# Layer norm inside a software-pipelined transformer stage: statistics and root moved from GpSimd to VectorE, ScalarE's part moved within its tick, output stored by batch

## The reference

```python
h = _layernorm(x)
for l in range(6):
    h = h + attn_layer(shift_tokens(h), Wqkv[l], q_scale[l], k_scale[l], Wo[l])
    h = h + ffn_layer(shift_tokens(h), ln_g[l], ln_b[l], W1[l], b1[l], W2[l], b2[l])
x = x + h

def ffn_layer(x, g, bln, W1, b1, W2, b2):
    mu = x.mean(-1, keepdims=True)
    var = ((x - mu) ** 2).mean(-1, keepdims=True)
    xn = (x - mu) / jnp.sqrt(var + 1e-05) * g + bln
    a, gate = jnp.split(xn @ W1 + b1, 2, -1)
    return a * jax.nn.gelu(gate, approximate=False) @ W2 + b2
```

## Time and profile before

| what | value |
|---|---|
| median of 3 runs | 2961.94 us (2951.48 to 2964.03) |
| profiled execution, own time | 2952.71 us |
| its span | 2950.9 us |
| mean granted TensorE clock | 0.936 of full speed |
| busy: PE, DVE, ACT, POOL | 88%, 59%, 53%, 49% of the span |
| last stage | from about 1815 us to the end |

### The profile page before, as it was taken

One profiled execution on the slowest core, in us unless ns is written; L12 is line 12 of the kernel. 1 busy time (PEld: TensorE's weight loads), 2 busy tenths in 40 slices (PEclk: granted clock), 3 DMA queues, 4 the chain that ended last, 5 costly groups with the idle time before them and its releaser, 6 DMA issues. The chain is left out here.

```text
span 2950.9 us, 59262 instructions
## 1 busy us (share of the span) xinstructions
PE 2591.2 (88%) x20009; PEld 1660.6 (56%) x20009; DVE 1740.3 (59%) x3832; ACT 1562.2 (53%) x5035; POOL 1434.5 (49%) x2340
## 2 busy tenths in 40 slices
PE   5999978898989979776689996999999999999996
PEld 3455545465645646554445553566666666666664
DVE  3466656546657655555545555766666667666662
ACT  1455536525747646532245553666665666666663
POOL 0344434203536613300024443877787777877772
PEclk8799998998979999987779998999999999999998
DMA  2000000010000000000000001010101101001000
GB/s 68 1 0 0 0 8 2 12 32 5 2 4 2 2 32 0 5 1 8 2 26 0 0 0 57 16 34 19 30 24 28 33 20 30 26 26 34 20 23 8
DMA packets 45612, 47.16 MB, mean 16 GB/s; under 512 B 11899, under 2 KB 31365, under 8 KB 45382
## 3 DMA queue, kind: packets, MB, share of 16 engines
q1 hardware_dynamic: 45382, 44.18, 5.3%
HBM read 31.05 MB, written 0.52 MB: 11 GB/s over the span
## 5 line engine op out<-in xcount | busy, mean ns | idle before, releaser
L1025 POOL TENSOR_TENSOR l_probs<-l_probs,rowinv 128x512 f32<-128x512 f32 (+2 forms) x256 | 192.4, 772 | 569.8 <-DVE rowinv L1037 569.0
L1045 DVE TENSOR_REDUCE negmax<-scores 128x1 f32<-128x508 f32 (+4 forms) x512 | 212.8, 467 | 220.1 <-PE scores L922 180.3
L2237 ACT ACTIVATE net_probs<-bank,net_negmax 128x96 f32<-128x96 f32 x768 | 250.9, 339 | 167.4 <-DVE net_negmax L2380 167.2
L2380 DVE TENSOR_REDUCE net_negmax<-bank 128x4 f32<-128x384 f32 x192 | 107.0, 557 | 319.6 <-PE bank L2085 318.9
L1025 POOL TENSOR_TENSOR lora_probs<-lora_probs,rowinv 128x508 f32<-128x508 f32 (+1 forms) x256 | 149.5, 617 | 255.2 <-DVE rowinv L1037 255.2
L2301 POOL TENSOR_TENSOR net_rope<-net_rope,net_sin_parts 128x512 f32<-128x512 f32 x192 | 243.8, 1270 | 9.6 <-DVE net_sin_parts L2356 9.6
L2309 POOL TENSOR_TENSOR net_probs<-net_probs,net_inverse 128x384 f32<-128x384 f32 x192 | 158.6, 826 | 153.4 <-DVE net_inverse L2363 153.4
L990 ACT ACTIVATE l_probs<-scores,negmax 128x512 f32<-128x512 f32 (+2 forms) x256 | 139.5, 550 | 167.8 <-DVE negmax L1045 167.0
L124 DVE COPY turned<-flip 128x512 f32<-128x512 f32 (+3 forms) x280 | 163.0, 582 | 74.2 <-PE flip L949 64.7
L2319 POOL TENSOR_TENSOR net_rope<-net_rope,net_head_inv 128x512 f32<-128x512 f32 x192 | 201.1, 1047 | 0.0
L737 DVE TENSOR_REDUCE negmax<-scores 128x2 f32<-128x256 f32 (+2 forms) x192 | 157.7, 822 | 65.8 <-PE scores L645 36.4
(11 more groups left out here) (426 smaller groups left out, 6471.3 us busy)
## 6 DMA issues: line engine op xcount, KB each, us to landing
net_w_qkv<-in_L_ffn_Wqkv SPq DMA_DIRECT2D x12, 768.0 KB, 5.7
net_vals_between<-net_vals SPq DMA_DIRECT2D x48, 192.0 KB, 2.5
net_w_out<-in_L_ffn_Wo SPq DMA_DIRECT2D x6, 512.0 KB, 4.2
net_vals_between<-net_vals SPq DMA_DIRECT2D x48, 64.0 KB, 1.9
moe_w<-in_L_ffn_w13T SPq DMA_DIRECT2D x8, 256.0 KB, 2.7
net_w<-in_L_ffn_W SPq DMA_DIRECT2D x6, 341.0 KB
moe_w<-in_L_ffn_w2T SPq DMA_DIRECT2D x8, 128.0 KB, 2.3
ctx_tok<-in_ctx SPq DMA_DIRECT2D x1, 768.0 KB, 6.6
```

Of the source, the lines that this page charges most:

```text
L1025: last = nc.gpsimd.tensor_tensor(own, own, rowinv[:, u * tail + w:u * tail + w + 1].to_broadcast([P, k1 - k0]), ALU.mult)
L1045: last = nc.vector.tensor_reduce(negmax[:, u * tail + w:u * tail + w + 1], scores[:, 2 * qt + h, k0:k1], AX.X, ALU.max, negate=True)
L2237: last = nc.scalar.activation(prob_blocks(g)[:, w, :], score_blocks(g)[:, w, :], ACT.Exp, bias=maxima[:, g % 4, w:w + 1], accum_out=sums[: ...
```

## The change

VectorE takes the statistics in LATE itself, right behind the copy of the late half, and makes the inverse root there (`root_of_variance`: eleven small operations that wait for each other, then the shift). GpSimd's root of the norm goes. ScalarE's low copy in LATE and its normalising in ZT move ahead of the exponentials of their tick, behind values' copy. In the last four jobs VectorE adds each batch to `x` as soon as its last sum is made, and SyncE stores that batch; `add_all` and `store` behind the stream go. Left out of the diff below are the argument lists without `ln_sum`, and the semaphores `finished` and `sent`.

```diff
@@ -1916,8 +1915,9 @@
             summed, stored = signal("net_summed", G), signal("net_stored", G)
             out_made, out_added = signal("net_out_made", JOBS), signal("net_out_added", JOBS)
             low_moved, late_made, late_moved = signal("net_low_moved", JOBS), signal("net_late_made", JOBS), signal("net_late_moved", JOBS)
-            measured, gathered, spread_in = signal("net_measured", 2 * JOBS), signal("net_gathered", 2 * JOBS), signal("net_spread", 2 * JOBS)
-            ln_rooted, normed = signal("net_ln_rooted", ROOT_OPS * JOBS), signal("net_normed", 2 * JOBS)
+            measured, gathered = signal("net_measured", 2 * JOBS), signal("net_gathered", 2 * JOBS)
+            LN_OPS = 11
+            ln_rooted, normed = signal("net_ln_rooted", LN_OPS * JOBS), signal("net_normed", 2 * JOBS)
             ln_shifted = signal("net_ln_shifted", JOBS)
             z_turned, z_moved = signal("net_z_turned", JOBS), signal("net_z_moved", JOBS)
             gates_made, gates_moved = signal("net_gates_made", JOBS), signal("net_gates_moved", 3 * JOBS)
...
@@ -2032,6 +2033,11 @@
                         if n is not None and n % B == B - 1 and n < JOBS - 1:
                             sp.wait_ge(down_made.sem, down_made.at(0, n + 1))
                             ffn_weights_in(n // B + 1)
+                        if n is not None and n >= JOBS - B:
+                            b = n % B
+                            sp.wait_ge(finished.sem, finished.at(0, b + 1))
+                            sp.dma_start(out[b].rearrange("(t p) d -> p t d", p=P), x[:, QT * b:QT * (b + 1), :]).then_inc(sent.sem, 16)
+                    sp.wait_ge(sent.sem, sent.at(0, B))
 
                 @block.tensor
                 def _(pe):
...
@@ -2228,6 +2234,19 @@
                             square(u, 1, k_filled)
                             act.wait_ge(v_filled.sem, v_filled.at(0, u + 1))
                             copy("act", vals[:, m % 3, t, half_cols(c)], v_bank).then_inc(v_copied.sem, 1)
+                        n = at_tick(s, LATE, PER, JOBS)
+                        if n is not None:
+                            l, b = job(n)
+                            own = slice(QT * b, QT * (b + 1))
+                            act.wait_ge(out_added.sem, out_added.at(0, n + 1))
+                            copy("act", z[:, own, 0:half], xin[:, own, 0:half]).then_inc(low_moved.sem, 1)
+                        n = at_tick(s, ZT, PER, JOBS)
+                        if n is not None:
+                            l, b = job(n)
+                            act.wait_ge(ln_shifted.sem, ln_shifted.at(0, n + 1))
+                            for q in range(QT):
+                                own = z[:, QT * b + q, :]
+                                affine("act", own, own, ln_inv[:, q:q + 1], ln_shift[:, q:q + 1]).then_inc(normed.sem, 1)
                         g = s
                         if 0 <= g < G:
                             act.wait_ge(maxed.sem, maxed.at(0, g + 1))
...
@@ -2243,12 +2262,6 @@
 
                             until(act, scored, g - 1)
                             copy("act", qk_T[:, g % 2, :, :].rearrange("p s n -> p (s n)"), turn_bank).then_inc(copied["act"].sem, 1)
-                        n = at_tick(s, LATE, PER, JOBS)
-                        if n is not None:
-                            l, b = job(n)
-                            own = slice(QT * b, QT * (b + 1))
-                            act.wait_ge(out_added.sem, out_added.at(0, n + 1))
-                            copy("act", z[:, own, 0:half], xin[:, own, 0:half]).then_inc(low_moved.sem, 1)
                         m = at_tick(s, SHIFT, PER, JOBS)
                         if m is not None:
                             l, b = job(m)
...
@@ -2257,10 +2270,6 @@
                         n = at_tick(s, ZT, PER, JOBS)
                         if n is not None:
                             l, b = job(n)
-                            act.wait_ge(ln_shifted.sem, ln_shifted.at(0, n + 1))
-                            for q in range(QT):
-                                own = z[:, QT * b + q, :]
-                                affine("act", own, own, ln_inv[:, q:q + 1], ln_shift[:, q:q + 1]).then_inc(normed.sem, 1)
                             if b == 0:
                                 act.wait_ge(ffn_in.sem, ffn_in.at(l, FFN_LOADS))
                             act.wait_ge(z_turned.sem, z_turned.at(0, n + 1))
...
@@ -2321,12 +2330,6 @@
                         if j is not None:
                             pool.wait_ge(reduced.sem, reduced.at(0, 2 * j + 2))
                             inverse_root(pool, head_sums[:, j % 2, :], 1e-24, head_inv[:, j % 2, :], head_temp, rooted, ROOT_OPS * j)
-                        n = at_tick(s, LATE + 1, PER, JOBS)
-                        if n is not None:
-                            pool.wait_ge(spread_in.sem, spread_in.at(0, 2 * n + 2))
-                            inverse_root(pool, ln_sum[:, :], LN_EPS, ln_inv[:, :], ln_temp, ln_rooted, ROOT_OPS * n)
-                            pool.wait_ge(ln_rooted.sem, ln_rooted.at(0, ROOT_OPS * (n + 1)))
-                            nc.gpsimd.tensor_tensor(ln_shift[:, :], ln_shift[:, :], ln_inv[:, :], ALU.mult).then_inc(ln_shifted.sem, 1)
                         u = at_tick(s, PROJ + 1, 2, S)
                         if u is not None:
                             add_parts(u, 0)
...
@@ -2356,24 +2359,30 @@
                         nc.vector.tensor_tensor(sin_parts[:, (2 * u + s) % 4, :].rearrange("p (h f d) -> p h f d", f=2, d=DH // 2), swapped, table,
                                                 ALU.mult).then_inc(parted.sem, 1)
 
+                    def root_of_variance(dve, n):
+
+                        lower, y, t = ln_temp[:, 0, :], ln_temp[:, 1, :], ln_temp[:, 2, :]
+                        done = [LN_OPS * n]
+
+                        def then(ins):
+                            done[0] += 1
+                            ins.then_inc(ln_rooted.sem, 1)
+                            dve.wait_ge(ln_rooted.sem, ln_rooted.at(0, done[0]))
+                        then(nc.vector.tensor_scalar(lower, meanvar[:, 0:QT, 1], LN_EPS, -0.5, ALU.add, ALU.mult))
+                        then(nc.vector.tensor_scalar(y.bitcast(I32), lower.bitcast(I32), -0.5, ROOT_MAGIC, ALU.mult, ALU.add))
+                        for r in range(3):
+                            then(nc.vector.tensor_tensor(t, y, y, ALU.mult))
+                            then(nc.vector.tensor_tensor(t, t, lower, ALU.mult))
+                            then(nc.vector.scalar_tensor_tensor(y if r < 2 else ln_inv[:, :], t, 1.5, y, ALU.add, ALU.mult))
+                        assert done[0] == LN_OPS * (n + 1)
+
+                        nc.vector.scalar_tensor_tensor(ln_shift[:, :], meanvar[:, 0:QT, 0], -1.0, ln_inv[:, :], ALU.mult, ALU.mult).then_inc(ln_shifted.sem, 1)
+
                     for s in TICKS:
                         g = s - 1
                         if 0 <= g < G:
                             dve.wait_ge(exped.sem, exped.at(0, g + 1))
                             nc.vector.reciprocal(inverse[:, g % 4, :], sums[:, g % 4, :]).then_inc(inverted.sem, 1)
-                        n = at_tick(s, LATE + 1, PER, JOBS)
-                        if n is not None:
-                            l, b = job(n)
-                            dve.wait_ge(late_moved.sem, late_moved.at(0, n + 1))
-                            dve.wait_ge(low_moved.sem, low_moved.at(0, n + 1))
-                            for q in range(QT):
-                                nc.vector.bn_stats(stats[:, q, :], z[:, QT * b + q, :]).then_inc(measured.sem, 1)
-                            for q in range(QT):
-                                dve.wait_ge(measured.sem, measured.at(0, 2 * n + q + 1))
-                                nc.vector.bn_aggr(meanvar[:, q, :], stats[:, q, :]).then_inc(gathered.sem, 1)
-                            dve.wait_ge(gathered.sem, gathered.at(0, 2 * n + 2))
-                            nc.vector.tensor_scalar(ln_sum[:, :], meanvar[:, 0:QT, 1], LN_EPS, None, ALU.add).then_inc(spread_in.sem, 1)
-                            nc.vector.tensor_scalar(ln_shift[:, :], meanvar[:, 0:QT, 0], -1.0, None, ALU.mult).then_inc(spread_in.sem, 1)
                         g = s
                         if 0 <= g < G:
                             dve.wait_ge(scored.sem, scored.at(0, g + 1))
...
@@ -2426,6 +2435,15 @@
                             l, b = job(n)
                             dve.wait_ge(late_made.sem, late_made.at(0, n + 1))
                             copy("dve", z[:, QT * b:QT * (b + 1), half:D], spare[:, 0:D].rearrange("p (t d) -> p t d", t=QT)).then_inc(late_moved.sem, 1)
+                            dve.wait_ge(late_moved.sem, late_moved.at(0, n + 1))
+                            dve.wait_ge(low_moved.sem, low_moved.at(0, n + 1))
+                            for q in range(QT):
```

(27 more changed lines are left out.)

## The result

The changed kernel takes 2929.24 us (median of 5 runs, 2919.78 to 2932.97) and the kernel before 2960.11 (5 runs, 2951.48 to 2964.03): a ratio of 0.9894, interval 0.9876 to 0.9911. The change makes the kernel 1.1% faster, some 31 us, where I had forecast 2967 and no measurable change. 2929 lies near the low end of my range. The profiled execution took 2919.78 us against 2952.71 before.

The account below looks back on a forecast made before the run. TensorE sets the pace, stalled 2.41 us in 22 jobs by ScalarE's normalising. Stall exchange +7.5, clock +9.4 and tail -4 make +13 on 2952.71, so 2965.6; stated as 2967 us, range 2922 to 2984.

Parts of the forecast that it names:

- The old stall: TensorE's transposes of the normed rows wait 2.41 us per job for ScalarE's normalising; ScalarE's new order alone removes this.
- the end of GpSimd's root: GpSimd loses the norm's root, some 4.2 us; costed at nothing, as TensorE doesn't wait for it in the steady part.
- The new one: TensorE stalls 2.75 us at values' projection (L2072), released by ScalarE's copy of the heads; +0.34 us per job net.
- The hold: A small root operation on VectorE waits for GpSimd's 1.27 us addition, making the maximum 2.87 us late instead of 1.7.
- ScalarE did not become second: Rival: exponentials behind the normalising delay the `qk_T` copy, so TensorE stalls twice a job; 2986 us, chance 0.18.
- The tail: Last job and end: earlier root 2.0 us, smaller sum and store 2.4, job 22 giving back up to 0.5; together -4.
- the store: At the end, last sum and store of one batch instead of four: gain between 1.7 and 3 us, taken as 2.4.
- VectorE's lateness: The root's chain on VectorE makes the next maximum 2.87 us late with the hold, 1.7 us without.
- the clock: TensorE's clock drops behind the stall in 16 of 22 jobs instead of 10, at 1.57 us each: +9.4 us.
- not held: Rival: VectorE's chain is not held behind GpSimd's addition, maximum only 1.7 us late; 2924 us, chance 0.27.

Follow-up runs that it names:

- the kernel with the addition first: Changed kernel with GpSimd's addition of the rotary parts placed ahead of the heads' inverse norms: 2902.97 us, ratio 0.9794 to the kernel before.
- the repeat: The changed kernel measured once more, without a further edit, beside the second group of runs: 2929.91 us, ratio 0.9901 to the kernel before.
- the kernel with four steps: Changed kernel with a fourth Newton step in the root, three more dependent operations on VectorE: 2990.88 us, ratio 1.0114 to the kernel before.

## Why the prediction was wrong

**What held.** The old stall went, but not as I had it: I wrote that ScalarE's order alone takes it away and costed the end of GpSimd's root at nothing. That order alone left 2.15 us of 2.41; it takes the earlier root as well. The change has both, so this error did not move the forecast. The new one came at values' projection, by ScalarE's copy of the heads, behind VectorE's maximum, once in each job and instead of the old one. The hold came in all 22 jobs. The Trainium skill, "SBUF — State Buffer", section "SBUF: two separate sides", has VectorE and GpSimd exclude each other for a whole instruction where VectorE's has two SBUF inputs and GpSimd's reads SBUF; here 22 of 22 chains show it, and the kernel with the addition first shows its price. ScalarE did not become second: the interval less the stall is 44.23 - 2.08 = 42.15 us, and 44.50 - 2.41 = 42.09 before, so no second wait of any size has come. The tail gave -7.4 where I had -4: ScalarE starts 2.36 us behind the root's first operation, not 2.54, and the store gave 3.0, above my 2.4 but within its bound; jobs 21 to 22 gave 1.5 where I allowed 0.5. That total leans on an undisturbed clock: in the repeat, with a drop between jobs 22 and 23, the tail gave only -3.2.

**The first wrong size: VectorE's lateness.** I had 2.87 us behind an old start, so a stall of 2.75 and +0.34 per job, +7.5 in all. (The sum's own rows make 2323.62 - 2320.77 = 2.85; the 0.02 doesn't matter.) The stall is 2.08 (2.24 in the seven jobs in which the third operation is held, as I had it), and the interval without a drop is shorter by 0.27 (by 0.11 in those), -4.8 in all. Measured on job 9 against the earlier trace rows, with the two executions laid on each other at the tick before (17.02 us apart), the maximum is late by 2.24, not 2.87. The parts are: the copy of `z` starts 0.16 earlier; a dependent step is 0.197 us and not 0.21, -0.14 over the chain; one operation more is through before GpSimd's addition begins (the fourth is held, not the third), -0.2; and the maximum starts 0.17 behind the last of the chain, not 0.27, -0.10. None is large; together they are 0.6 us, and turn the sign. The 0.34 was the difference of two stalls of 2.4 and 2.75, and the errors of the terms in it were 0.1 to 0.2 each.

**The second, and larger: the clock.** I took ten drops in 22 at 2.41 us, put "between 10 and 22" at 2.75 and added 9.4 us. With the stall at 2.08 the clock gave back some 12.6 in the profiled execution: 2 jobs of 22 have a drop instead of 10, for 0.3 us less stall. The term's slope was right in sign and far too flat. The table shows a steep place: 0 to 3 jobs of 22 with a drop up to 2.24 us, 10 at 2.41, 21 at 2.68, and there most cost 2.9 us. With my own stall of 2.75 the time would have been no 2967: the kernel with four steps has 2.68 and takes 2990.88. So 2967 was also wrong for the stall that it assumed. What the term needed was to be priced at both ends of the stall's uncertainty; the sign of the whole hung on whether the stall came out above or below the old one.

**The range.** 2922 to 2984 held 2929 by luck: only because the rival "not held" had its place near there, by another mechanism: the chain is held, and the time comes from a shorter lateness and from the clock.

**Open.** How many drops the timed runs have isn't seen; the two profiled executions have 2 and 3. Jobs 0 to 21 and the tail together give -27.1 and -21.1 us in these, against medians of -31 and -25; where the rest lies isn't shown. That a smaller stall goes with fewer drops is shown by every row of the table, with the stall at either of the two places. Why one of the same length is followed by a drop in some jobs and not in others was not tried. Nor was the 7.5 us between the starts of the stage.

## What to carry to other kernels

When an edit exchanges one stall for another of nearly its size, the difference is what must be worked out, and everything that hangs on it by a steep slope is to be priced at both ends of its uncertainty; here 0.3 us per job decided between 1% faster and 1% slower, through TensorE's clock. A chain of tiny dependent operations should be placed away from GpSimd's long instructions: exchanging two blocks of code on GpSimd was worth 0.9 us per job, where the change itself had won 0.3 (at full clock). And where two pieces of work hide behind each other, as ScalarE's order and GpSimd's root do, each alone is worth little or harms, so a chain is followed until something that isn't late is found.

## What the runs showed of the hardware

- Small operations of VectorE wait for GpSimd's: a `tensor_tensor` of 128x2 took 1.12 to 1.19 us instead of 0.16 behind an addition of 1.27 us, in each of the 22 jobs; the `tensor_scalar` of the earlier trace rows, of one tensor and as small, took 1.15 behind one. Beside GpSimd's operations of 128x32 (0.25 us) the longest operation of the chain was 0.27, and 0.23 with the addition first.
- Dependent operations of 128x2 on VectorE with a semaphore between them start 0.197 us apart.
- The granted clock's answer to one stall per job is steep: no drop in 22 jobs up to 1.65 us, 2 or 3 at 2.04 to 2.24, 10 at 2.41, 21 at 2.68.
- A fall of the clock has no one price: 1.4 to 1.7 us at stalls up to 2.41, 2.9 at 2.68, where it stays low for about twice as long.
